# Four changes to the order of work in an attention kernel's first stages: exponentials ahead of a tile's own copy, a product ahead of the projection, reciprocals ahead of the second norm's low half, bias sums on GpSimd

## The chip, the cores and the metric

One core of a Trainium2 chip. The metric is the device time of one execution in microseconds; before the change it is 941.41 us, the median of three runs (941.12 to 943.48).

## The reference, cut to what matters

`x` and `ctx_1024` are (8, 512, 512), float32. Two blocks follow one another, each with a residual:

```python
x = x + xattn(layernorm(x), ctx, ctx, W_proj, b_proj)
x = x + ffn(layernorm(x), wf, uf, bf, wi, ui, bi, wc, uc, bc, wo, uo, bo, in_c)
```

- `xattn`: 16 heads of 32 columns. Scores of queries and keys are scaled by 32 to the power -1/2, masked to a distance of at most 64 positions, put through a softmax and multiplied with the values; `y @ W_proj.T + b_proj` follows.
- `ffn`: a recurrence over the batch axis of 8 steps on a state `c` of (512 rows, 512 columns), starting from `in_c` broadcast to all rows; then the output.

```python
def step(c, xt):
    ft = sigmoid(xt @ wf.T + c @ uf.T + bf)
    it = sigmoid(xt @ wi.T + c @ ui.T + bi)
    gt = tanh(xt @ wc.T + c @ uc.T + bc)
    return ft * c + it * gt, None
h = tanh(x @ wo.T + c_final @ uo.T + bo)
```

## The kernel before, in words

The kernel is one instruction stream for each engine, and all streams walk one list, `steps` (lines 114 to 328). The list is written out by a loop over slots. Each engine takes from it the steps that concern it, in the list's order, and waits on semaphores where it needs another engine's result. So the place of a step in the list is its place in the queue of every engine that does a part of it.

**Tiles and slots.** There are 32 tiles of 128 positions (4 for each of 8 batch elements), and each tile has 4 slots, one for a group of 4 heads: slot n belongs to tile i = n // 4 with s = n % 4. The attention of a slot is made of these steps:

- `score` (PE line 730, 16 small matmuls into the four banks `ps_a`; DVE line 1012 scales, masks and copies to `probs`, and takes the row's minimum, four instructions, one for each head),
- `exp` (ACT line 900, four exponentials, each with its row sum),
- `turn` (PE transposes, lines 742 or 752; ACT line 905 copies the result to `probs_t`; up to slot 19 DVE line 1033 copies a second half),
- `sides` (from slot 20 on: DVE line 1047, 32x32 transposes of what the tile sees of its neighbours),
- `recip` (DVE line 1023, reciprocals of the row sums; POOL line 667 spreads them over the columns of `recip`),
- `value` (PE lines 766, or 773 and 778).

Slots up to 19 are called `early` in the code; from slot 20 on to slot 35 come single slots with products of the recurrence between them; from slot 36 on slots go in pairs.

**Once for each tile.** `ln1`/`ln1b` are the first norm, `bias` (POOL line 647) adds the projection's bias to the row, `query`/`query_out` turn the normed tile. `spread` (s = 3) turns the reciprocals: PE line 796, then ACT line 909 copies them from the bank `ps_m` to `tile_row`. `mult` (DVE line 1054) multiplies the attention's result with them, and `halves` (ACT line 913, POOL line 662) splits the product in a high and a low part. `proj` (s = 0 of the next tile: PE line 805, from tile 5 on lines 683 to 685) is the projection. `resid` and `stat2` (DVE, POOL line 672), then `ln2b` (DVE line 1082) make the second norm. `turn2` (s = 2 of the tile after) turns that normed tile for the recurrence: PE line 820 transposes it into `ps_m`, ACT line 930 copies the high part from there, and DVE line 1098 makes the low part from `ps_m` and the high part, so it waits for ACT's copy.

**The recurrence.** `cell` is one product of three matmuls of 512 columns (lines 683 to 685). 48 of them (12 gates) belong to the first step, from slot 19 on; `gate` (ACT line 947) takes a finished sum, `blend` and `state` follow (DVE, ACT).

**The first step's biases.** The state's share of the first step is the same for all rows. `row` (PE line 788) computes it in slots 5, 13 and 17, `column` (DVE line 1110) turns it to columns in `column_t`, which lies in the tile `gate`, and `column_sum` (DVE lines 1116 and 1119) adds both of its columns to `bias`. The first gate of each kind waits for its own sum (line 942).

**Weights.** `split` (ACT line 936) and `rest` (POOL line 652, two subtractions of 128x512, each) split the gates' weights in the early slots.

The order in a slot, as it matters here (lines 244 to 306):

- early: `turn n`, `exp n+1`, `score n+2`, then for s = 2 `turn2`, `value n`, `column_sum`, `rest`, `recip n+1`.
- slots 20 to 35: `turn n`, two products (a gate behind the first or the second where it ends a sum), then `query`, `turn2` or `spread`, then `score n+2`, `mult`, `exp n+1`, `value n`, `recip n+1`, `sides n+1`; for s = 0 then `ln1b`, `bias`, `proj`, `resid`, `stat2`; and one product at the end.

Two waits tie a slot to the ones around it. A `turn` from slot 20 on writes to the bank `ps_a0`, so PE waits until DVE has taken the first head of the scores of the next slot from it:

```python
pe.wait_ge(masked, HPG * (i + 1) + 1)      # line 749, turn i
```

And `value n` waits for DVE's transposes of `sides n` (line 757), `value` of a tile's first slot also for `mult` of the tile before (line 760).

## Time and profile before

| | |
|---|---|
| median of 3 runs | 941.41 us |
| the profiled execution, its own time | 941.73 us |
| its span, first to last instruction | 939.8 us |
| granted TensorE clock over the span | 1.000, the level of 2.4 GHz |
| PE busy | 919.0 us (98%) |
| DVE busy | 675.9 us (72%) |
| ACT busy | 476.2 us (51%) |
| POOL busy | 204.8 us (22%) |

The profile shows one execution. Busy time of PE counts a matmul from its start to its modelled end, and ends overlap the next start, so gaps between matmuls are seen better in the time from start to start. What ends the time of the kernel is read from waits: the idle time of an engine ahead of an instruction, and the engine that released it.

### The profile page before, as it was taken

To read this page: it belongs to the slowest core of one execution; us is meant where nothing else is said; L and a number is where in the kernel's file an instruction comes from. 1 tells how busy PE (TensorE), PEld (TensorE's weight loads), DVE (VectorE), ACT (ScalarE), POOL (GpSimd) and SP (SyncE) were. 2 spreads that over 40 slices of the span, in tenths; PEclk is the share of its full clock that TensorE was granted. 3 is DMA by queue.
4 is the path that set the end of the run, shared out by engine and by line. 5 is a ranking of instruction groups with operands and counts; after the bars stand their busy time and mean duration, and the time that the engine had idled before them with its cause. 6 is when DMAs were issued, how large, how long until landed. Compare 5 with 4: busy or idle time off the path is not lost.

```text
span 939.8 us, 21981 instructions
## 1 busy us (share of the span) xinstructions
PE 919.0 (98%) x7842; PEld 715.6 (76%) x7842; DVE 675.9 (72%) x2281; ACT 476.2 (51%) x1430; POOL 204.8 (22%) x228
## 2 busy tenths in 40 slices
PE   7999999999999999999999999999999999999998
PEld 5555567677887788887887888788777888888887
DVE  6888898888779977998799878987798531143222
ACT  6888666655565544554465555555555421131222
POOL 5475322211110111111111111111111100003444
PEclk9999999999999999999999999999999999999999
DMA  9564223224443443434543444434333150049862
GB/s 303 163 195 150 85 80 108 74 81 128 133 131 119 129 133 93 140 109 123 133 146 110 119 116 123 108 109 109 98 98 91 50 165 0 1 178 371 324 235 101
DMA packets 139348, 123.58 MB, mean 131 GB/s; under 512 B 46824, under 2 KB 104168, under 8 KB 137704
## 3 DMA queue, kind: packets, MB, share of 16 engines
q1 hardware_dynamic: 138520, 121.91, 42.8%
q8 instruction: 63, 1.03, 0.5%
q10 hardware_dynamic: 720, 0.27, 0.2%
q14 instruction: 45, 0.37, 0.1%
HBM read 87.70 MB, written 34.46 MB: 130 GB/s over the span
## 4 chain that ended last, share of the span: by engine, by line
PE 87%; DVE 6%; issue 3%; ACT 2%; DMA 1%; POOL 1%; SPq 0%; DVEq 0%; POOLq 0%; ACTq 0%
PE ps_g L683 18%; PE ps_g L685 17%; PE ps_g L684 17%; PE ps_a L730 5%; PE ps_a L752 5%; PE ps_m L683 3%; PE ps_v L773 3%; PE ps_m L685 3%; PE ps_m L684 3%; PE ps_m L805 2%; PE ps_a L685 2%; PE ps_a L683 2%; PE ps_a L684 2%; PE ps_v L778 2%; DVE probs L1012 2%
## 5 line engine op out<-in xcount | busy, mean ns | idle before, releaser
L900 ACT ACTIVATE probs<-probs,rowmin 128x192 f32<-128x192 f32 (+1 forms) x512 | 239.4, 470 | 114.4 <-DVE rowmin L1012 114.4
L1012 DVE CUSTOM_DVE_ANT_0 probs<-ps_a,mask 128x192 f32<-128x192 f32 (+1 forms) x512 | 166.0, 386 | 30.0 <-PE ps_a L730 28.8
L683 PE MATMUL ps_g<-state_hi,gate_w 128*128 128x512 f32 x336 | 133.6, 398 | 0.0
L685 PE MATMUL ps_g<-state_hi,gate_w 128*128 128x512 f32 x336 | 131.1, 390 | 0.0
L684 PE MATMUL ps_g<-state_lo,gate_w 128*128 128x512 f32 x336 | 130.8, 389 | 0.0
L1047 DVE STREAM_TRANSPOSE keys<-probs 32x128 f32<-32x128 f32 x420 | 125.6, 299 | 5.2
L947 ACT ACTIVATE gate<-ps_g,bias 128x512 f32<-128x512 f32 x84 | 57.6, 686 | 105.6 <-PE ps_g L685 105.2
L900 ACT ACTIVATION_READ_ACCUMULATOR probs<-probs,rowmin 128x1 f32 x512 | 96.3, 188 | 0.0
L662 POOL TENSOR_TENSOR attn_lo<-recip,attn_hi 128x512 fp32r<-128x512 f32 x23 | 29.8, 1294 | 276.8 <-ACT attn_hi L913 276.8
L905 ACT ACTIVATE probs_t<-ps_a 128x512 f32<-128x512 f32 x108 | 59.3, 595 | 50.9 <-PE ps_a L752 50.9
L683 PE MATMUL ps_g<-x2t_even,gate_w 128*128 128x512 f32 x192 | 80.0, 417 | 0.0
L683 PE MATMUL ps_g<-x2t_odd,gate_w 128*128 128x512 f32 x192 | 76.9, 401 | 0.0
L685 PE MATMUL ps_g<-x2t_even,gate_w 128*128 128x512 f32 x192 | 75.2, 392 | 0.0
L684 PE MATMUL ps_g<-x2t_even,gate_w 128*128 128x512 f32 x192 | 75.0, 391 | 0.0
L685 PE MATMUL ps_g<-x2t_odd,gate_w 128*128 128x512 f32 x192 | 74.9, 390 | 0.0
L684 PE MATMUL ps_g<-x2t_odd,gate_w 128*128 128x512 f32 x192 | 74.8, 390 | 0.0
L685 PEld LDWEIGHTS ps_g<-state_hi,gate_w 128*128 128x128 f32 x336 | 63.1, 188 | 13.4
L683 PEld LDWEIGHTS ps_g<-state_hi,gate_w 128*128 128x128 f32 x336 | 63.1, 188 | 12.6
L684 PEld LDWEIGHTS ps_g<-state_lo,gate_w 128*128 128x128 f32 x336 | 63.2, 188 | 12.3
L730 PE MATMUL ps_a<-keys,queries 32*64 32x192 f32 (+1 forms) x2048 | 62.3, 324 | 2.8 <-DVE rowmin L1012 2.0
L752 PE MATMUL ps_a<-ident,probs 128*128 128x128 f32 x432 | 60.4, 274 | 1.4 <-ACT probs L900 0.7
L752 PEld LDWEIGHTS ps_a<-ident,probs 128*128 128x128 f32 x432 | 51.0, 139 | 13.1 <-ACT probs L900 3.9
(218 smaller groups left out, 1722.6 us busy)
## 6 DMA issues: line engine op xcount, KB each, us to landing
values<-ctx_rows SPq DMA_DIRECT2D x34, 256.0 KB, 4.4
xr<-x SPq DMA_DIRECT2D x32, 256.0 KB, 3.6
keys<-ctx_t SPq DMA_DIRECT2D x16, 512.0 KB, 4.0
x_dram<-xr SPq DMA_DIRECT2D x32, 256.0 KB, 2.6
gate_w<-x2t_dram SPq DMA_DIRECT2D x8, 1024.0 KB, 9.3
keys<-ctx_t SPq DMA_DIRECT2D x16, 384.0 KB, 3.5
x2t_dram<-x2t_even SPq DMA_DIRECT2D x12, 512.0 KB, 4.3
x2t_dram<-x2t_odd SPq DMA_DIRECT2D x12, 512.0 KB, 4.4
```

The source lines that it names most:

```text
L662: pool.tensor_tensor(attn_lo[:, :, :], attn if i < SENT else recip[:, :, :], attn_hi[:, :, :].bitcast(F32), ALU.subtract)\
L683: pe.matmul(ps, lhs[0], rhs[0], start=start, stop=False)
L684: pe.matmul(ps, lhs[0], rhs[1], start=False, stop=False)
L685: return pe.matmul(ps, lhs[1], rhs[0], start=False, stop=stop)
L730: mm = pe.matmul(ps_a[h][q, score_at[i] + k.start:score_at[i] + k.stop], queries[rows, g, q], keys[rows, key_home[tile], g, k], start=True ...
L752: mm = pe.transpose(ps_turn[i][:, h * P:(h + 1) * P], probs[:, i % 2, h, own:own + P], ident[:, :])
L773: pe.matmul(ps_v[HEAD * h:HEAD * (h + 1), g * P:(g + 1) * P], values[:, tile % 2, 0, d], own_home[i][:, h, :], start=True, stop=False)
L900: act.activation(row, row, ACT.Exp, bias=rowmin[:, i % 2, h:h + 1], scale=-1.0, accum_out=rowsum[:, i // G % 2, i % G, h:h + 1]).then_inc( ...
L905: act.activation(own_home[i], ps_turn[i][:, :].rearrange("p (a q) -> p a q", a=HPG), ACT.Copy)\
L947: act.activation(gate[:, min(gt, 1), :], ps_g[i % 2][:, :], ACT.Tanh, bias=(first_bias if b == 0 else bias)[:, gt, m:m + 1], scale=1.0 if ...
L1012: dve.tensor_tensor_reduce(probs[:, i % 2, h, 0:SEEN[t]], ps_a[h][:, score_at[i]:score_at[i] + SEEN[t]], mask[:, MASK0[t]:MASK0[t] + SEEN[ ...
L1047: turn = dve.transpose(side_home[i][BLK * keys_of:BLK * (keys_of + 1), :, q], probs[q, i % 2, :, col:col + BLK])
```

## The change

In the list of steps:

- In the early slots with s = 2, `recip n+1` comes ahead of `turn2` (and so ahead of `column_sum` and `rest` on GpSimd).
- In slots 20 to 35, `exp n+1` comes directly behind the two products, ahead of `query`, `turn2` or `spread`.
- In slots 20 to 35 with s = 0, the product from the slot's end comes ahead of `proj`.

And `column_sum` goes from VectorE (two instructions) to GpSimd (two for the first gate kind, three for the others); every gate of the first step waits for all three sums.

```diff
         elif not early:
             cells(2)
+            if n + 1 < SLOTS:
+                steps.append(("exp", n + 1))
             if s > 0:
                 tile_steps((None, "query", "turn2", "spread")[s], (None, i + 1, i - 1, i)[s])
         if n + 2 < SLOTS:
             steps.append(("score", n + 2))
         if s == 1:
             tile_steps("ln2b", i - 1)
+        recip_first = early and s == 2
+        if recip_first:
+            steps.append(("recip", n + 1))
         if s == 3 and i >= WHOLE:
             tile_steps("mult", i)
         if early:
             tile_steps(("proj", "query", "turn2", "spread")[s], (i - 1, i + 1, i - 1, i)[s])
-        elif n + 1 < SLOTS:
-            steps.append(("exp", n + 1))
...
         if n + 1 < SLOTS:
-            steps.append(("recip", n + 1))
+            if not recip_first:
+                steps.append(("recip", n + 1))
...
             if not early:
+                cells(1)
                 tile_steps("proj", i - 1)
...
         if n >= FIRST_CELL:
-            cells(PER_SLOT[min((n - FIRST_CELL) // (TT * G), B - 1)] - 2)
+            cells(PER_SLOT[min((n - FIRST_CELL) // (TT * G), B - 1)] - (2 if s > 0 else 3))
...
             for kind, i in steps:
+                if kind == "column_sum":
+                    pool.wait_ge(column_turned, i + 1)
+                    pool.wait_ge(bias_half, 1)
+                    row = first_bias[:, i, :]
+                    pool.tensor_tensor(row, column_t[:, :, 0], column_t[:, :, 1], ALU.add).then_inc(column_sum, 1)
+                    pool.wait_ge(column_sum, (1, 2, 4)[i])
+                    if i > 0:
+                        pool.tensor_tensor(row, row, half[:, :].to_broadcast([P, G]), ALU.mult).then_inc(column_sum, 1)
+                        pool.wait_ge(column_sum, (1, 3, 5)[i])
+                        pool.tensor_tensor(row, bias[:, i, :], row, ALU.subtract).then_inc(biased, 1)
+                    else:
+                        pool.tensor_tensor(row, row, bias[:, i, :], ALU.add).then_inc(biased, 1)
...
                     if b == 0:
-                        act.wait_ge(biased, gt + 1)
+                        act.wait_ge(biased, NG)
...
-                if kind == "column_sum":
-                    dve.wait_ge(column_turned, i + 1)
-                    dve.wait_ge(bias_half, 1)
-                    scale = 0.5 if i else 1.0
-                    dve.scalar_tensor_tensor(out=first_bias[:, i, :], in0=column_t[:, :, 0], scalar=scale,
-                                             in1=bias[:, i, :], op0=ALU.mult, op1=ALU.add).then_inc(column_sum, 1)
-                    dve.wait_ge(column_sum, i + 1)
-                    dve.scalar_tensor_tensor(out=first_bias[:, i, :], in0=column_t[:, :, 1], scalar=scale,
-                                             in1=first_bias[:, i, :], op0=ALU.mult, op1=ALU.add).then_inc(biased, 1)
```

## Rows read from the trace of the kernel before

**Rows 1.** Windows by stage; columns: busy us and instructions of each engine, clock, DMA.
```profile
20.00:92.00 72.00, 66.63 (x788) 37.93 (x787) 60.99 (x230) 59.81 (x192) 42.67 (x53) 1.00 0.55 176
92.00:186.00 94.00, 88.28 (x907) 61.75 (x904) 79.92 (x302) 63.08 (x191) 25.20 (x38) 1.00 0.30 86
186.00:700.00 514.00, 512.96 (x4704) 411.31 (x4703) 432.15 (x1477) 274.08 (x861) 81.35 (x83) 1.00 0.43 119
```

**Rows 2.** Waits of PE from 20 to 92 us: us in total, times, longest.
```profile
PE ps_m L796 <- POOL recip L667: 2.3, 4, 1.2
```

**Rows 3.** Waits of PE from 92 to 186 us.
```profile
PE ps_a L752 <- ACT probs L900: 0.7, 4, 0.2
```

**Rows 4.** Waits of DVE from 92 to 186 us.
```profile
DVE probs L1012 <- PE ps_a L730: 5.4, 4, 1.7
DVE x2t_odd L1098 <- ACT x2t_odd L930: 3.7, 4, 1.6
```

**Rows 5.** Timeline, slots 22 and 23: start, us, engine, line, shapes, idle before.
```profile
107.08 0.69 ACT L947 ACTIVATE gate<-ps_g,first_bias 128x512 f32<-128x512 f32 x1
...
108.21 0.60 ACT L930 ACTIVATE x2t_odd<-ps_m 128x512 fp32r<-128x512 f32 x1 [0.44 <-PE ps_m L820]
...
108.71 0.50 ACT L900 ACTIVATE probs<-probs,rowmin 128x256 f32<-128x256 f32 x1
...
108.84 0.69 DVE L1098 TENSOR_TENSOR x2t_odd<-ps_m,x2t_odd 128x512 fp32r<-128x512 f32 x1 [0.17 <-ACT x2t_odd L930]
...
109.20 0.50 ACT L900 ACTIVATE probs<-probs,rowmin 128x256 f32<-128x256 f32 x1
...
109.45 0.41 DVE L1012 CUSTOM_DVE_ANT_0 probs<-ps_a,mask 128x256 f32<-128x256 f32 x1
...
110.21 0.94 PE L752 MATMUL ps_a<-ident,probs 128*128 128x128 f32 x4
```

**Rows 6.** Timeline, slot 24: the sides and the value product behind them.
```profile
117.69 1.85 DVE L1047 STREAM_TRANSPOSE probs_t<-probs 32x128 f32<-32x128 f32 x6
...
119.65 0.42 PE L773 MATMUL ps_v<-probs_t,values 128*32 128x128 f32 x8 [1.20 <-issue]
```

**Rows 7.** Timeline of ACT, slot 30: the first exponential.
```profile
151.81 0.45 ACT L900 ACTIVATE probs<-probs,rowmin 128x192 f32<-128x192 f32 x1
```

**Rows 8.** Timeline, slot 31: gate, spread copy and multiplication.
```profile
155.47 0.69 ACT L947 ACTIVATE gate<-ps_g,first_bias 128x512 f32<-128x512 f32 x1 [0.79 <-PE ps_g L685]
...
156.06 0.59 ACT L909 ACTIVATE tile_row<-ps_m 128x512 f32<-128x512 f32 x1
...
157.56 0.69 DVE L1054 TENSOR_TENSOR tile_row<-ps_v,tile_row 128x512 f32<-128x512 f32 x1
```

**Rows 9.** Timeline of PE, slot 28: start of the projection.
```profile
141.23 0.47 PE L683 MATMUL ps_m<-proj_w,attn_hi 128*128 128x512 f32 x1 [0.29 <-POOL attn_lo L662]
```

**Rows 10.** Timeline of ACT, slot 20: the first gate.
```profile
101.72 0.69 ACT L947 ACTIVATE gate<-ps_g,first_bias 128x512 f32<-128x512 f32 x1 [4.72 <-PE ps_g L685]
```

**Rows 11.** Timeline of DVE, slot 18: the bias sum and the reciprocal behind it.
```profile
89.81 0.15 DVE L1116 SCALAR_TENSOR_TENSOR first_bias<-gate,bias 128x4 f32<-128x4 f32 x1
...
90.07 0.18 DVE L1023 RECIPROCAL invsum<-rowsum 128x4 f32<-128x4 f32 x1
```

**Rows 12.** Timeline, slots 11 and 12.
```profile
56.65 0.66 PE L796 MATMUL ps_m<-ident,recip 128*128 128x128 f32 x4 [1.17 <-POOL recip L667]
...
58.04 0.69 DVE L1054 TENSOR_TENSOR tile_row<-ps_v,tile_row 128x512 f32<-128x512 f32 x1
...
59.31 3.70 PE L805 MATMUL ps_m<-state,tile_row 128*128 128x512 f32 x8
```

**Rows 13.** Lines 667 and 672 on POOL: ns min/median/max, first and last start.
```profile
L667 POOL COPY recip<-invsum x36: 282/292/523, 11.7 to 174.8; 128x128 f32<-128x128 f32 x36
L672 POOL TENSOR_TENSOR moments<-moments,half x32: 549/550/559, 32.8 to 762.1; 128x1 f32<-128x1 f32 x32
```

**Rows 14.** Line 1082 on DVE: ns min/median/max, first and last start.
```profile
L1082 DVE TENSOR_SCALAR tile_row<-xr,moments x32: 543/546/1096, 34.1 to 764.2; 128x512 f32<-128x512 f32 x32
```

## The prediction

> **What bounds the kernel now.** I first cut the span into stages with the windows [rows 1]. From 186 to 700 us PE is busy in 513 of 514 us: there PE alone sets the pace, and whatever an earlier stage gains or loses goes to the end undiminished. The whole change lies ahead of that, in the early slots (20 to 92 us) and the single slots (92 to 186 us). In these two stages PE is idle for 5.4 and 5.7 us, DVE is busy for 85% of both, and ACT for 83 and 67%. So here two or three engines take turns in holding each other up. The views of waits say who. In the early slots PE's largest wait is the transposes of reciprocals, for GpSimd [rows 2]. In the single slots PE waits little for exponentials [rows 3], and DVE waits four times for ACT's copy of the high part, once for each `turn2` (slots 22, 26, 30, 34) [rows 4]. That last row is the one that I look at hardest, because the change puts four exponentials ahead of this copy on ACT.
>
> **Exponentials first, s = 2 (four slots).** Today, in slot 22, ACT does a gate at 107.08, is idle, copies the high part at 108.21 as soon as PE has it, and then does the exponentials at 0.49 us each [rows 5]. DVE takes the low part at 108.84, 0.63 us after the copy began, and the scores of slot 24 behind it, at 109.45. In the list `turn2` stands ahead of `score n+2`, so on DVE nothing passes the low part. With the change ACT starts the exponentials behind the gate (0.60 us from a gate's start to the next one's, [rows 8]): the copy starts 0.60 + 4 x 0.49 = 2.56 us behind the gate's start instead of 1.13. That is 1.43 us later, and so are the low part and all that DVE does after it. (By durations rather than starts it would be 0.69 + 2.0 - 1.13 = 1.56.) In slots 26, 30 and 34 gate and copy start the same 1.13 us apart. In slots 30 and 34 the exponentials have 192 columns and are 0.45 us long [rows 7], by the same overlap 0.44 from start to start: 0.60 + 1.76 - 1.13 = 1.23 us.
>
> Is this on the path? DVE has no gap of 0.1 us between the low part of slot 22 and the end of its transposes in slot 24, at 119.54, and PE stands idle for 1.20 us before the value product at 119.65, which needs them [rows 6]. So the whole 1.43 us reaches PE there. Slot 26 is the same up to slot 28, 1.43 us. There the projection waits 0.29 us for its split operand [rows 9]; the product moved ahead of it covers that, so 1.43 - 0.27 = 1.16 us stay. In slot 30 DVE is 1.23 us late, and a second thing comes on top.
>
> **Exponentials first, s = 3.** In slots 23, 27, 31 and 35 they pass the copy of `spread`, which `mult` needs. In slot 31 the copy starts at 156.06 and `mult` at 157.56 [rows 8]. PE is some 0.8 us late there (below), so the gate starts at 156.27, the exponentials at 156.87, the copy at 158.63, and with its 0.59 us `mult` comes at 159.2, 1.65 us late, more than the 1.23 by which DVE is late anyway. The value product of slot 32 shows no wait for DVE today, so some of that is slack: between 1.23 and 1.65 I take 1.4 us for this tile. In slots 23 and 27 DVE's own delay is the larger, so nothing is added; in slot 35 both give about 1.3 us. What the step wins is that the transposes of a slot wait less for its exponentials: the four of slot 23 are drawn out to 0.94 us [rows 5], of which some 0.3 is waiting. That gain is inside the sum, since PE then waits for DVE instead. Sum of both: 1.43 + 1.16 + 1.4 + 1.3 = 5.3 us lost.
>
> In slots with s = 0 or 1 no ACT work stands between the old place and the new one: zero. The cover is that ACT has only a query copy there, and that stays behind.
>
> **The product ahead of `proj` (s = 0, four slots).** PE does the same work in another order. It fills a wait only in slot 28, counted above. The price is that `resid` gets its sum 0.69 us later (three matmuls of 0.23 us). DVE is idle in these slots before the next scores, four times and 5.4 us together [rows 4], and that hides it; with that gone it would cost up to 0.69 a tile. The first gate comes ahead of `split_proj` on ACT; ACT is idle for 4.72 us before that gate [rows 10]. Zero.
>
> **Bias sums off DVE (slots 6, 14, 18).** Two instructions leave DVE: 89.81 to 90.07 is 0.26 us [rows 11]. In each of these slots DVE works without a gap up to `mult`, on which PE then waits, so 3 x 0.26 = 0.8 us gained. On GpSimd 2, 3 and 3 small additions come in. No row shows one of 128x4; the nearest are the copy of 0.29 us and the power of 0.55 [rows 13]. I take 0.3, so up to 1 us a sum with its waits. Behind them in GpSimd's queue are `rest` and the next `ln1`; the splits that `rest` makes are read by the third row product, three slots later, and SP's loads into the freed buffers are split later still. Zero, and 0.5 us at most. All gates now wait for all three sums, which are made in slot 18, before the first gate at 101.72 [rows 10]. Zero.
>
> DVE instructions can be slowed by GpSimd: the second norm takes 0.55 us as a rule and 1.10 at most [rows 14], the long ones begin while GpSimd subtracts weights. What follows the moved sums on DVE reads PSUM or a single tensor, and such copies and statistics are equally long with and without GpSimd at work beside them, so I add nothing. The Trainium skill, page "SBUF — State Buffer", section "Who interferes with whom", says that GpSimd and a VectorE instruction with two SBUF inputs (or in a two-port mode) exclude one another, the later one blocking fully. By that rule the new additions may hold DVE for their own length, and by it the sums' gain could turn into a loss.
>
> **Reciprocals first (slots 2, 6, 10, 14, 18).** On DVE the reciprocal and the low part change places, which fills 0.1 us in slot 14, where DVE waits for the high part. On GpSimd the spreading no longer stands behind `rest`, and PE's waits for it, 2.3 us in four slots [rows 2], go. Three of them hide behind DVE, which must reach `mult` before the projection can start. In slot 10 it is different: the wait of 1.17 us delays value, transposes and scores one after another, until `proj` at 59.31; `mult` starts at 58.04 and needs 0.62 + 0.05 us, so `proj` could start at 58.7 [rows 12]: 0.6 us gained. Bounds: 0.1 us in all if DVE takes it back, 2.3 if every wait falls out. Sum of the two early parts: 0.8 + 0.1 + 0.6 = 1.5 us gained.
>
> **The sum.** 5.3 - 1.5 = +3.8 us. The profiled execution took 941.73 us (a span of 939.8 and 1.9 around it), 0.3 above the median; 945.5 against it is 945.2 against the median of 941.41. That is 0.4% slower; 0.3%, or 2.8 us, is about what a measurement of this kernel can tell from no change.
>
> **Rivals.**
> - *Turns only* (0.16). DVE catches up in its idle time before the next value product, and PE pays only at the transposes: in slot 23 they need the first masked score, 109.45 + 1.43 + 0.41 = 111.3 instead of 110.21, less the 0.3 us of waits that vanish, 0.8 us. Four times, less 0.3 and 1.5: +1.4, 942.8 us. For it: DVE's longest wait before the low part is 1.6 us [rows 4], so it isn't always full. Against: that idle time lies ahead of the delay, not behind it.
> - *No stall* (0.12). The copy's delay is hidden after all, and the transposes' waits for exponentials, up to 0.3 us in eight slots, are won: -2.4 - 0.3 - 1.5 = -4.2, 937.2 us. This is the side where it is faster. It decides if DVE's low part is not what the next scores wait behind. For it: PE's waits on L900 are real. Against: the order in the list, and rows 4, which show DVE already waiting there.
> - *Nothing moves in the single slots* (0.08): the exponentials, though first in line, find their masked scores late and end as before. Then only the early gain stays, 939.9 us. Against: DVE has those scores done a whole slot earlier.
> - *GpSimd holds DVE* (0.08). At the three sums DVE loses 0.3 us instead of winning 0.26: 945.2 + 3 x 0.56 = 946.9 us. That is the page's rule from above; rows 14 bear out that such blocking occurs here, but for another kind of instruction.
> - The forecast has the rest, 0.56. Its own range is 943.6 (5.3 lost, 0.8 + 2.3 won) to 947.2 (nothing won, and the longer durations).
>
> So slower 0.56 + 0.08, within 0.3% 0.16 + 0.08, faster 0.12. The range of 942.3 to 947.3 us takes in the forecast, the first rival and the last, and leaves out 0.20.
>
> **What the profile after would show.** Right: DVE's wait before L1098 grows from 3.7 to about 9 us; PE gets a wait of about a microsecond at L752 in slots 23, 27, 31 and 35, released by L1012; the wait before the value product of slot 24 grows from 1.2 to some 2 us; the waits of L796 on L667 are gone; L1116 and L1119 run on POOL; from 186 us on all is alike, shifted. Wrong: slot 36 starts earlier than now, the copy L930 starts within 1.2 us of its gate as before, or DVE waits for its high part no longer than now.

## The result, and the profile after

In a comparison of nine executions each, the changed kernel takes 944.61 us in the median (943.93 to 947.66) and the kernel before 941.12 us. The ratio is 1.0041, with a 95% interval from 1.0032 to 1.0051: slower by about 0.4%, more than the 0.3% that can be told from no change. The forecast was 945.2 us, with a range of 942.3 to 947.3.

The profiled execution took 946.33 us (span 944.4 us). It is not the median one, and it began late: its slot 0 already starts 0.88 us behind that of the profile before. Such starts differ from one execution to the next (up to 1.1 us in the profiles below), so all shifts below are counted from slot 0 on. Over the span, PE is busy for 920.0 us, DVE for 674.8, ACT for 476.3 and POOL for 206.1, each within 1.3 us of before. The work is the same; only its order has moved.

The windows by stage, their bounds moved a little with the work (busy us and instructions of PE, PE's weight loads, DVE, ACT and POOL; clock; DMA share and GB/s):

```profile
20.00:91.00 71.00, 67.53 (x804) 38.28 (x796) 60.41 (x227) 59.95 (x194) 44.90 (x61) 1.00 0.55 176
91.00:190.00 99.00, 87.16 (x902) 60.82 (x898) 80.53 (x302) 63.84 (x194) 24.99 (x37) 1.00 0.29 83
190.00:704.00 514.00, 512.84 (x4700) 410.99 (x4696) 431.25 (x1477) 274.14 (x861) 81.53 (x83) 1.00 0.43 118
```

Against [rows 1], PE's idle time fell in the early slots (5.4 us of 72 before, 3.5 of 71 now) and grew in the single slots (5.7 of 94, now 11.8 of 99). From 190 us on there is 1.2 us idle in 514, as before. The waits of DVE and of PE from 90 to 192 us (us in total, times, longest) name the place:

```profile
DVE x2t_odd L1115 <- ACT x2t_odd L947: 8.2, 4, 2.8
DVE probs L1029 <- PE ps_a L747: 2.3, 3, 1.0
DVE tile_row L1013 <- PE ps_m L822: 2.0, 1, 2.0
```

```profile
PE ps_a L769 <- DVE rowmin L1029: 3.5, 4, 1.1
PE ps_a L747 <- ACT probs_t L922: 2.2, 3, 0.8
PE ps_a L769 <- ACT probs L917: 0.5, 3, 0.2
```

Lines of PE, DVE and ACT stand 17 further down than before: L1115 is the low part of `turn2` (L1098 before), L947 ACT's copy of the high part (L930), L769 the transposes (L752), L747 the scores (L730), L1029 DVE's masked scores (L1012). DVE's wait for the copy went from 3.7 us [rows 4] to 8.2, and PE's transposes now wait for DVE, 3.5 us in four slots, where they waited only for exponentials before [rows 3]. DVE's idle time ahead of the masked scores, behind which the working hid several things, shrank from 5.4 us to 2.3. Slot 22 in the timeline (start, us, engine, line, shapes, idle time before and its releaser) is to be read against [rows 5]:

```profile
106.36 0.69 ACT L964 ACTIVATE gate<-ps_g,first_bias 128x512 f32<-128x512 f32 x1
...
106.94 0.50 ACT L917 ACTIVATE probs<-probs,rowmin 128x256 f32<-128x256 f32 x1
...
108.42 0.49 ACT L917 ACTIVATE probs<-probs,rowmin 128x256 f32<-128x256 f32 x1
...
108.91 0.57 ACT L947 ACTIVATE x2t_odd<-ps_m 128x512 fp32r<-128x512 f32 x1
...
109.52 0.69 DVE L1115 TENSOR_TENSOR x2t_odd<-ps_m,x2t_odd 128x512 fp32r<-128x512 f32 x1 [0.86 <-ACT x2t_odd L947]
...
110.13 0.41 DVE L1029 CUSTOM_DVE_ANT_0 probs<-ps_a,mask 128x256 f32<-128x256 f32 x1
...
110.60 0.66 PE L769 MATMUL ps_a<-ident,probs 128*128 128x128 f32 x4 [0.26 <-DVE rowmin L1029]
```

The copy starts 108.91 - 106.36 = 2.55 us behind the gate, where it was 1.13; the working had 2.56. The low part, the masked scores and PE's transposes hang one behind the other as before: the first two steps are 0.6 us apart, and the transposes start 0.5 us behind the first masked score. The transposes have shrunk from 0.94 to 0.66 us: what they waited for exponentials is gone, and in its place they start later. In slot 31 the other half of the move shows, against [rows 8]:

```profile
157.96 0.69 ACT L964 ACTIVATE gate<-ps_g,first_bias 128x512 f32<-128x512 f32 x1 [0.79 <-PE ps_g L702]
...
160.30 0.58 ACT L926 ACTIVATE tile_row<-ps_m 128x512 f32<-128x512 f32 x1
...
160.98 0.69 DVE L1071 TENSOR_TENSOR tile_row<-ps_v,tile_row 128x512 f32<-128x512 f32 x1 [0.49 <-ACT tile_row L926]
```

Gate to copy is 2.34 us instead of 0.59, and `mult` now waits for the copy. In the early slots the wait of [rows 12] is gone, and the sums run on POOL in 0.2 us each (timeline, slots 11 and 18):

```profile
55.90 0.66 PE L813 MATMUL ps_m<-ident,recip 128*128 128x128 f32 x4
...
89.25 0.20 POOL L645 TENSOR_TENSOR first_bias<-gate 128x4 f32<-128x4 f32 x1
```

**Where the time came and went.** The table gives, for each kernel, by how many us ACT's copy behind the transposes of a slot starts later than in the kernel before, less the same number for slot 0. Negative is earlier. The kernels other than "after" are the experiments below; each one's name stands in the heading of its section.

| kernel | slot 14 | 20 | 22 | 24 | 26 | 28 | 30 | 32 | 36 |
|---|---|---|---|---|---|---|---|---|---|
| after | -1.02 | -1.30 | -1.62 | -0.21 | -0.22 | 1.18 | 0.83 | 2.54 | 3.71 |
| no_exp_first | -1.03 | -1.31 | -1.60 | -1.02 | -1.02 | -1.03 | -1.37 | -1.36 | -1.49 |
| exp_first_only | 0.01 | 0.02 | 0.02 | 1.44 | 3.01 | 4.40 | 4.37 | 6.07 | 7.41 |
| exp_first_s2 | -0.99 | -1.27 | -1.56 | -0.15 | 1.32 | 2.71 | 2.38 | 3.50 | 4.50 |
| exp_first_s2_behind | -1.03 | -1.31 | -1.60 | -0.88 | -0.88 | -0.59 | -0.94 | -0.93 | -1.31 |
| exp_first_s3 | -1.01 | -1.29 | -1.58 | -1.01 | 0.59 | 0.85 | 0.53 | 1.46 | 1.82 |
| exp_first_s3_filled | -1.00 | -1.30 | -2.30 | -1.73 | -2.31 | -2.06 | -2.54 | -1.60 | -1.54 |
| turn2_behind_score | -1.02 | -1.31 | -1.61 | -0.89 | 0.58 | 0.86 | 0.52 | 1.16 | 1.20 |
| no_product_ahead | -1.01 | -1.30 | -1.61 | -1.60 | -1.60 | -1.61 | -1.60 | -1.60 | -1.60 |
| product_before_value | -1.03 | -1.31 | -2.31 | -1.73 | -2.33 | -2.33 | -2.81 | -2.81 | -2.72 |
| split_later | -1.00 | -1.30 | -2.30 | -2.29 | -2.88 | -2.88 | -3.36 | -3.36 | -3.25 |
| no_recip_first | -0.36 | -0.56 | -0.87 | -0.29 | -0.29 | -0.30 | -0.64 | -0.63 | -0.75 |
| sums_on_dve | -0.73 | 0.94 | 0.88 | 1.45 | 3.02 | 3.01 | 2.69 | 2.69 | 2.57 |

The changed kernel is 1.3 us ahead at slot 20 and 3.7 us behind at slot 36; from there to slot 80 its shift moves by 0.3 us, and at the end of the span it is 3.7 again. That the later stage passes a shift on unchanged holds here, but not in every kernel: no_exp_first, 1.49 us ahead at slot 36, ends its span 2.7 us ahead. The kernel before has a PE wait of 0.6 us for a second norm at 673 us, which the profiled execution of no_exp_first doesn't have. So a difference between spans of about a microsecond can't be put down to the edited slots alone. A loss comes in each stretch with an s = 2 slot and the slot behind it, and in some stretches PE wins something back (28 to 30: -0.35).

### The profile page after: what moved, and what is told of

The parts are those of the page before. It is cut to its first block, busy times and chain, and to the rows that moved or that the text cites. A ratio compares the mean times of both kernels' runs of the same rounds, so it can differ in the third digit from the quotient of the medians.

```text
span 944.4 us, 21983 instructions
## 1 busy us (share of the span) xinstructions
PE 920.0 (97%) x7842; PEld 716.0 (76%) x7842; DVE 674.8 (71%) x2275; ACT 476.3 (50%) x1430; POOL 206.1 (22%) x236
## 3 DMA queue, kind: packets, MB, share of 16 engines
q8 instruction: 63, 1.03, 0.5%
## 4 chain that ended last, share of the span: by engine, by line
PE 85%; DVE 7%; ACT 3%; issue 3%; DMA 2%; SPq 0%; POOL 0%; DVEq 0%; ACTq 0%
PE ps_g L700 17%; PE ps_g L702 17%; PE ps_g L701 17%; PE ps_a L747 5%; PE ps_a L769 4%; PE ps_m L700 3%; PE ps_v L790 3%; PE ps_m L702 3%; PE ps_m L701 3%; PE ps_m L822 2%; DVE probs L1029 2%; PE ps_a L702 2%; PE ps_a L701 2%; PE ps_a L700 2%; ACT probs L917 2%
## 5 line engine op out<-in xcount | busy, mean ns | idle before, releaser
L1029 DVE CUSTOM_DVE_ANT_0 probs<-ps_a,mask 128x192 f32<-128x192 f32 (+1 forms) x512 | 166.0, 386 | 28.7 <-PE ps_a L747 27.1
L747 PE MATMUL ps_a<-keys,queries 32*64 32x192 f32 (+1 forms) x2048 | 62.7, 325 | 3.9 <-ACT probs_t L922 2.2
L769 PE MATMUL ps_a<-ident,probs 128*128 128x128 f32 x432 | 58.4, 273 | 4.1 <-DVE rowmin L1029 3.5
L769 PEld LDWEIGHTS ps_a<-ident,probs 128*128 128x128 f32 x432 | 50.5, 139 | 15.1 <-DVE rowmin L1029 5.9
```

The lines of the kernel that those rows point to most:

```text
L747: mm = pe.matmul(ps_a[h][q, score_at[i] + k.start:score_at[i] + k.stop], queries[rows, g, q], keys[rows, key_home[tile], g, k], start=True ...
L769: mm = pe.transpose(ps_turn[i][:, h * P:(h + 1) * P], probs[:, i % 2, h, own:own + P], ident[:, :])
L1029: dve.tensor_tensor_reduce(probs[:, i % 2, h, 0:SEEN[t]], ps_a[h][:, score_at[i]:score_at[i] + SEEN[t]], mask[:, MASK0[t]:MASK0[t] + SEEN[ ...
```

## The experiments

The theory was that of the prediction: exponentials passing ACT's copy of the high part hold DVE's low part and the scores queued behind it. The rivals were that the loss comes from the passing of `spread`'s copy, from the product ahead of `proj`, or from GpSimd's new work. Line numbers differ by a few from kernel to kernel; the tiles named in a row tell which step it is. "Before" was measured anew beside each group of kernels: 941.66, 941.58 and 941.86 us.

### All but the exponentials' move (no_exp_first)

```diff
         elif not early:
             cells(2)
-            if n + 1 < SLOTS:
-                steps.append(("exp", n + 1))
...
             tile_steps(("proj", "query", "turn2", "spread")[s], (i - 1, i + 1, i - 1, i)[s])
+        elif n + 1 < SLOTS:
+            steps.append(("exp", n + 1))
```

> The changed kernel with the exponentials of slots 20 to 35 back in their old place; reciprocals first, the sums on GpSimd and the product ahead of the projection stay. Theory (the exponentials delay ACT's copy of the high part, DVE stands still on it, and 5.3 us of the loss is this): only the early gain of 1.5 to 1.6 us and up to 0.3 in slot 28 stay, 939.3 us against 941.1 of before, and DVE waits 3.7 us at the four high parts as before. Rival (the other three parts cost the time, most likely GpSimd's sums holding DVE up): near the changed kernel, 944 us.

Measured: 940.24 us, ratio 0.9986 (0.9977 to 0.9995). The theory had 939.3 us, the rival 944. DVE waits 3.6 us at the high parts, about as before. Slot 36 comes 1.49 us ahead of before instead of 3.71 behind. So the exponentials' move costs 5.2 us of the path, and the other three edits together win 1.5. They don't win it all where the prediction had it: at slot 22 the kernel is 1.60 ahead, at slot 24 only 1.02. The cause is in the timeline of slot 21:

```profile
102.60 0.55 POOL L689 TENSOR_TENSOR moments<-moments,half 128x1 f32<-128x1 f32 x1 [0.44 <-DVE moments L1089]
103.11 2.55 POOL L674 TENSOR_TENSOR proj_w<-state,proj_w 128x512 fp32r<-128x512 f32 x2
...
103.33 0.42 DVE L1029 CUSTOM_DVE_ANT_0 probs<-ps_a,mask 128x256 f32<-128x256 f32 x1
...
104.36 1.58 DVE L1099 TENSOR_SCALAR tile_row<-xr,moments 128x512 f32<-128x512 f32 x1
```

The second norm on DVE takes 1.58 us, three times its usual 0.55 and longer than the 1.10 of [rows 14]. It begins during GpSimd's subtractions of `split_proj` and ends at 105.94, 0.3 us behind their end at 105.66. In the kernel before the two ends stand 0.3 us apart as well (105.95 + 0.86 on DVE, 104.00 + 2.52 on POOL). DVE had its scores done earlier, but the norm could not use that: both times it ends 0.3 us behind GpSimd's second subtraction. The masked scores beside the same subtractions take 0.42 us each, as everywhere else in these slots, so not every DVE instruction is held; split_later below moves the subtractions away and tests the reading.

### Only the exponentials' move (exp_first_only)

```diff
         elif not early:
             cells(2)
+            if n + 1 < SLOTS:
+                steps.append(("exp", n + 1))
...
-        elif n + 1 < SLOTS:
-            steps.append(("exp", n + 1))
```

> The kernel before with the exponentials' move alone. Theory: the whole loss and none of the early gain, +5.3 us or 946.4 us, DVE waits 8 to 9 us at the four high parts. Rival (the other parts cost the time): 941 us, or below it by up to 2.4 us of waits for exponentials.

Measured: 948.44 us, ratio 1.0068 (1.0055 to 1.0082), 7.41 us behind at slot 36; 946.4 us were expected. The first round, slots 22 to 24, costs 1.42 us; the prediction said 1.43. DVE waits 8.9 us for the copy, PE's transposes 4.2 us for DVE. But 1.57 us fall between slots 24 and 26, where no theory had a loss. That is the clock, shown below with exp_first_s3. Without it, 5.8 us: some more than the 5.2 from the other side, since here the norm of slot 21 takes 0.87 us, as in the kernel before, and the first round counts in full: DVE's wait ahead of the low part of slot 22 is 1.58 us, against 0.17 + 1.43 of the prediction.

### Exponentials first, but not in s = 2 (exp_first_s3)

```diff
-            if n + 1 < SLOTS:
+            if s != 2 and n + 1 < SLOTS:
                 steps.append(("exp", n + 1))
             if s > 0:
                 tile_steps((None, "query", "turn2", "spread")[s], (None, i + 1, i - 1, i)[s])
+            if s == 2 and n + 1 < SLOTS:
+                steps.append(("exp", n + 1))
```

> The changed kernel, but in slots with s = 2 the exponentials stand behind turn2 again; in slots with s = 3 they stay ahead of the copy of spread. Theory: DVE's wait at the high part is back to 3.7 us and with it all of the loss goes; ahead of spread the exponentials save up to 0.5 us in each of four tiles: 938 to 939.5 us. Rival (the late copy of spread makes the multiplication late, and that is the loss): 943 to 944 us.

Measured: 943.12 us, ratio 1.0011 (1.0000 to 1.0021). The theory had 938 to 939.5 us, so it missed, and the number is the rival's (943 to 944). DVE's wait for the high part is 3.6 us, as in [rows 4]; so that stall belongs to s = 2 alone. Yet this kernel is 2.9 us slower than no_exp_first. Two waits show why (DVE, then PE, 91 to 190 us; L928 copies the spread reciprocals, L924 the transposed scores):

```profile
DVE tile_row L1073 <- ACT tile_row L928: 1.5, 3, 0.8
```

```profile
PE ps_a L749 <- ACT probs_t L924: 2.4, 3, 0.8
```

Everything that ACT does behind the exponentials is late in the s = 3 slots: the copy for `mult`, the splits, and the next `probs_t`, for which PE's scores wait. Against no_exp_first the stretches 26 to 28, 30 to 32 and 34 to 36 lose 0.27, 0.92 and 0.53 us, 1.7 together. The move was meant to shorten waits here, and in these slots it costs.

The remaining 1.6 us fall between slots 24 and 26 again (-1.01 to 0.59). PE's timeline (some rows left out):

```profile
117.26 0.59 PE L749 MATMUL ps_a<-keys,queries 32*64 32x192 f32 x16 [0.83 <-ACT probs_t L924]
119.05 0.42 PE L792 MATMUL ps_v<-probs_t,values 128*32 128x128 f32 x8 [1.20 <-DVE probs_t L1066]
...
120.99 0.63 PE L702 MATMUL ps_m<-proj_w,attn_hi 128*128 128x512 f32 x1
121.42 0.63 PE L703 MATMUL ps_m<-proj_w,attn_hi 128*128 128x512 f32 x1
...
124.08 0.39 PE L702 MATMUL ps_m<-proj_w,attn_hi 128*128 128x512 f32 x1
124.31 0.39 PE L703 MATMUL ps_m<-proj_w,attn_hi 128*128 128x512 f32 x1
```

And the window from 119 to 124 us (columns as above, the clock behind POOL):

```profile
119.00:124.00 5.00, 4.95 (x28) 3.90 (x29) 4.41 (x17) 1.29 (x3) 0.57 (x2) 0.66 0.00 0
```

Behind two idle stretches of 0.83 and 1.20 us, eight matmuls follow one another at 0.43 us instead of 0.23, and the granted clock of the stretch is 0.66, a mix of 1.2 and 2.4 GHz. 8 x 0.20 = 1.6 us lost. It doesn't happen in each execution. Eight of the eleven have a mean clock of 0.998 and take 942.2 to 944.6 us; the other three (1.000 or 0.999) take 940.7 to 940.9.

### The high part's copy and low part behind the scores (turn2_behind_score)

```diff
-            if s > 0:
+            if s in (1, 3):
                 tile_steps((None, "query", "turn2", "spread")[s], (None, i + 1, i - 1, i)[s])
         if n + 2 < SLOTS:
             steps.append(("score", n + 2))
+        if s == 2 and not early:
+            tile_steps("turn2", i - 1)
```

> The changed kernel, but in slots 22, 26, 30 and 34 turn2 comes behind score n+2 in the list, for PE, ACT and DVE; the exponentials stay ahead of its copy. Theory (what costs is that DVE's scores stand behind the low part's wait, not that the copy is late): DVE does the scores during the exponentials, no stall is left, and the waits for exponentials are won too: 937 to 939.5 us. Rival (the late copy itself costs, since spread must wait for the low part, or ACT is what bounds these slots): 943 to 945 us, with the wait at another instruction.

Measured: 942.05 us, ratio 1.0002 (0.9993 to 1.0011). All exponentials are first here, as in the changed kernel, but on DVE the scores no longer stand behind the low part. The wait shrinks to this:

```profile
DVE x2t_odd L1117 <- ACT x2t_odd L949: 1.2, 3, 0.5
```

Slot 36 is 1.20 us behind before instead of 3.71, and a clock fall of 1.47 us between slots 24 and 26 is in that (the mean clock is 0.997 or 0.998 in seven of eleven executions). Without it slot 36 would be 0.3 us ahead, so the queue behind the low part had cost 4.0 us. That queue was the cause of most of the loss. The median missed the 937 to 939.5 us of the theory: the cost of s = 3 stays, and the clock comes on top.

### Only s = 2 first, in both orders (exp_first_s2, exp_first_s2_behind)

exp_first_s2 is no_exp_first with the exponentials ahead of `turn2`:

```diff
         elif not early:
             cells(2)
+            if s == 2 and n + 1 < SLOTS:
+                steps.append(("exp", n + 1))
...
-        elif n + 1 < SLOTS:
+        elif s != 2 and n + 1 < SLOTS:
             steps.append(("exp", n + 1))
```

> The kernel of no_exp_first with the exponentials ahead of turn2 in slots with s = 2 alone, turn2 ahead of the scores as in the change; it completes the four cases (neither, s = 3, s = 2, both). Theory (DVE's stall at the high part is on the path whole, and behind it the late copy of spread is hidden): 1.43, 1.43, 1.2 and 1.2 us in the four tiles, slot 36 some 5.0 us later than in no_exp_first, or nearly all of what both together lose; 944.3 us. Rival (the two add up, 1.7 us being of spread): 3.5 us later, 942.8 us.

exp_first_s2_behind has the same, and `turn2` behind `score` by the edit of turn2_behind_score:

> The kernel of no_exp_first, and only in slots with s = 2 are the exponentials ahead of turn2, which comes behind score n+2; in slots with s = 3 they stay behind the copy of spread. From turn2_behind_score, which won nothing, and exp_first_s3, which lost 1.5 us beside no_exp_first. Theory (passing the copy of spread makes the multiplication late, in three or four tiles, and passing the high part's copy costs nothing once the scores are ahead of it): at no_exp_first or up to 1 us below it, 938.5 to 939.5 us. Rival (the exponentials ahead of the high part still cost): 941 us.

Measured: 945.11 us, ratio 1.0035 (1.0022 to 1.0049), for the first; 940.55 us, 0.9992 (0.9983 to 1.0000), for the second. The two differ by one place in the list. In the first, the changed kernel's two waits come back to the tenth:

```profile
DVE x2t_odd L1117 <- ACT x2t_odd L949: 8.2, 4, 2.8
```

```profile
PE ps_a L771 <- DVE rowmin L1031: 3.5, 4, 1.1
```

By slot 36 it loses 4.50 + 1.49 = 5.99 us to no_exp_first. 1.47 of it fall between slots 24 and 26, the clock again, so s = 2 costs 4.5 us (0.9 us by slot 24, 1.4 from 26 to 28, 1.1 from 30 to 32 and 1.2 from 34 to 36). The expectation had 5.0 us if the late copy of `spread` hides behind the stall, 3.5 if the two halves add up, so 4.5 lies between the two. The second kernel loses only 0.18 us to no_exp_first by slot 36; its median missed the 938.5 to 939.5 us of the theory, and five of its eleven executions have a mean clock of 0.998. With s = 3 (1.7) the sum of the two halves is 6.2, more than the 5.2 of both together: where DVE is late through s = 2, lateness of `spread` is partly hidden.

### Without the product ahead of the projection (no_product_ahead)

```diff
             if not early:
-                cells(1)
                 tile_steps("proj", i - 1)
...
-            cells(PER_SLOT[min((n - FIRST_CELL) // (TT * G), B - 1)] - (2 if s > 0 else 3))
+            cells(PER_SLOT[min((n - FIRST_CELL) // (TT * G), B - 1)] - 2)
```

> The kernel of no_exp_first (all parts but the exponentials' move) with the product put back behind the projection as well: reciprocals first and the sums on GpSimd alone. In no_exp_first the second norm of slot 21 took 1.58 us beside GpSimd's split of the projection's weights, and 0.7 us of the early gain went there. Theory (the product ahead of the projection delays DVE and GpSimd there, and the norm then waits for GpSimd): the reciprocal of slot 22 comes 1.6 us earlier than before the change instead of 0.9, but slots 28 and 32 win 0.3 and 0.1 us less; time 939.6 us, about that of no_exp_first. Rival (that norm's 1.58 us has nothing to do with the product): slot 22 as in no_exp_first, 0.9 us early, and 0.4 us slower in the end.

Measured, on the basis of no_exp_first: 939.24 us, ratio 0.9979 (0.9970 to 0.9987). The shift stays at -1.60 from slot 22 to 36. So the product ahead costs 0.6 us in slot 20 and wins back 0.35 us in slot 28 and 0.1 in slot 32, where it fills the projection's wait. The way of the loss can be followed: the projection of slot 20 comes 0.7 us later, DVE waits 2.0 us for it (L1013 above; 1.3 in the kernel before), so `stat2` and GpSimd's subtractions behind it come later, and the second norm ends with them. On balance the edit loses 0.1 us of the path. (The medians are 1.0 us apart; four of eleven executions of no_exp_first have a mean clock of 0.998, of this one a single one.)

### Reciprocals back behind; sums back on DVE (no_recip_first, sums_on_dve)

```diff
-        recip_first = early and s == 2
+        recip_first = False
```

> The kernel of no_exp_first with the reciprocals back behind the low half in the early slots. Theory: what they win is in slots 10 to 12 alone, 0.6 us, and a tenth in slot 14, so the lead over the kernel before at the end of slot 12 is 0.3 us instead of 1.0, and the time is 0.7 us above no_exp_first, 940 us. Rival (all of PE's waits of 2.3 us for the reciprocals count): 1.6 us above it, with a loss at each of slots 7, 11, 15 and 19.

Measured: 940.69 us, ratio 0.9993 (0.9983 to 1.0002). From slot 14 on it stands about 0.7 us behind no_exp_first: that is what the reciprocals' place is worth. The sums on GpSimd are left with 0.56 us at slot 20.

The other one puts the two DVE instructions of `column_sum` and the gates' waits back as before the change, and keeps the reciprocals first:

```diff
-                if kind == "column_sum":
-                    pool.wait_ge(column_turned, i + 1)
...
-                        act.wait_ge(biased, NG)
+                        act.wait_ge(biased, gt + 1)
...
+                if kind == "column_sum":
+                    dve.wait_ge(column_turned, i + 1)
```

> The kernel of no_exp_first with the bias sums back on DVE. Theory (0.26 us of DVE's time at each of the three sums is on the path to mult): later by 0.26 us from slot 8 on, 0.5 from slot 16, 0.8 from slot 20, so 0.8 us above no_exp_first, 940.1 us. Rival (GpSimd's two or three additions hold DVE up for as long as the sums took): no difference, or a gain.

Measured: 945.19 us, ratio 1.0037 (1.0023 to 1.0050), where 940.1 was expected: a gain of 0.3 us for each sum can't give the 4.1 us by which slot 36 is later than in no_exp_first. Against no_exp_first, 0.3 us is lost by slot 14 as expected, then 2 us more behind slot 14. Slot 14 in the timeline, POOL and DVE:

```profile
71.49 2.50 POOL L657 TENSOR_TENSOR gate_w<-early_w,gate_w 128x512 fp32r<-128x512 f32 x2
...
71.89 0.90 DVE L1121 SCALAR_TENSOR_TENSOR first_bias<-gate,bias 128x4 f32<-128x4 f32 x1
...
72.82 1.19 DVE L1124 SCALAR_TENSOR_TENSOR first_bias<-gate,first_bias 128x4 f32<-128x4 f32 x1
...
73.94 0.67 DVE L1038 COPY probs_t<-ps_g 64x512 f32<-64x512 f32 x1
```

Two additions on four columns take 0.90 and 1.19 us. In the kernel before they took 0.15 and 0.16 in all three slots, and here they do so in the other two. In the kernel before, the pair of subtractions of this slot ended at 72.47, just ahead of the first sum at 72.55. With the reciprocals first, GpSimd starts its pair of subtractions (71.49 to 73.99) just ahead of them; the first sum ends at 72.79, where the first subtraction should end (71.49 + 1.25 = 72.74), and the second at 74.01, with the second subtraction. Then DVE's `probs_t` is late, and the value product waits 1.7 us for it. So the reciprocals' move needs the sums' move. At slot 20 the sums' move alone gives -0.56 us, the reciprocals' move alone +0.94, and both -1.31. (The further 1.6 us between slots 24 and 26 is the clock again; its mean is 0.996 to 0.998 in all five executions.)

The Trainium skill, page "SBUF — State Buffer", section "Who interferes with whom", says that a VectorE instruction with two SBUF inputs and a GpSimd one that reads SBUF exclude each other, and that the one that starts later is fully blocked. These rows agree with it, in duration and in where the blocking ends.

### Another place for the product (product_before_value, exp_first_s3_filled)

```diff
             steps.append(("exp", n + 1))
+        if s == 0 and not early:
+            cells(1)
         if n < SLOTS:
             steps.append(("value", n))
...
             if not early:
-                cells(1)
                 tile_steps("proj", i - 1)
```

> The kernel of no_exp_first, but the product that was moved ahead of the projection goes one step further, ahead of value n in slots 20, 24, 28 and 32. PE stands idle there for 1.5, 1.2, 0.3 and 0 us. Theory: its 0.69 us fill that idle time in slots 20 and 24 and 0.3 in slot 28, the projection of slot 20 isn't delayed any more, and TensorE's clock falls less often behind the shorter idle time: about 1.5 us below no_exp_first, 938 us. Rival (DVE's transposes bound these slots, and the projection behind has to wait for its split operand instead): as no_exp_first, 939.3 us.

Measured, on the basis of no_exp_first: 938.36 us, ratio 0.9968 (0.9956 to 0.9981), slot 36 at -2.72; 938 was expected. PE used to be idle ahead of the value products of the s = 0 slots (slot 24 in [rows 6]); the same three matmuls fill that time there, and the wait of 1.20 us in slot 24 is down to 0.31.

The same edit on exp_first_s3 tests the reading of the clock, since it fills the idle 1.20 us ahead of the fall:

> The kernel of exp_first_s3 with the product that stood ahead of the projection moved on ahead of value n, into PE's idle time. In exp_first_s3 PE stood idle for 0.8 and 1.2 us in slot 24, and in 8 of 11 runs the clock was granted at 0.998 of full speed; in the profiled one it was at 1.2 GHz for 3.4 us just behind that idle time, and 1.6 us were lost. Theory (the idle time brings the clock down): granted clock 1.000 or 0.999 in nearly all runs, and 2.5 to 3 us below exp_first_s3, 940 to 940.6 us. Rival (the clock falls whatever PE does there): 0.998 as often as before, and only the 1.3 us of the filled wait won, 941.8 us.

Measured: 939.82 us, ratio 0.9978 (0.9969 to 0.9987), 3.3 us below exp_first_s3. All eleven executions have a mean clock of 1.000 or 0.999. The same window as above, and PE's wait ahead of the value product of slot 24:

```profile
119.00:124.00 5.00, 5.00 (x34) 3.84 (x39) 4.83 (x16) 2.04 (x9) 1.59 (x2) 1.00 0.00 0
```

```profile
117.89 0.43 PE L793 MATMUL ps_v<-probs_t,values 128*32 128x128 f32 x8 [0.30 <-issue]
```

The wait of 0.83 us ahead of the scores is still there; that of 1.20 us is down to 0.30, and the clock stays at 2.4 GHz. Of the 3.36 us between the two profiled executions at slot 36, 1.6 are the clock's, and the rest came with the work that was moved into the gap. By whole executions the rest is smaller: the three of exp_first_s3 at a mean clock of 0.999 or 1.000 are about 1 us above the median here.

The other runs bear the reading out. With the second wait filled (exp_first_s3_filled, product_before_value, split_later) none of 21 executions has a mean clock below 0.999. In every kernel whose profile shows that wait at its 1.20 us, some have. How many goes only roughly with the wait ahead of the scores: 9 of the 70 executions of the kernel before that were measured beside the experiments (0.37 us), 4 of 11 of no_exp_first (0.60), 8 of 11 of exp_first_s3 (0.83), but also all five of sums_on_dve (0.59) and only two of nine of the changed kernel (0.83). So the first wait doesn't decide alone, and why one execution falls and the next doesn't stays open.

### GpSimd's subtractions a slot later (split_later)

On top of product_before_value, the second pair of `split_proj` moves on GpSimd (not on ACT) to the slot behind:

```diff
         if FIRST_CELL <= n < FIRST_CELL + 2:
-            steps.append(("split_proj", PAIR * (n - FIRST_CELL)))
+            steps.append(("round_proj", PAIR * (n - FIRST_CELL)))
+        if n in (FIRST_CELL, FIRST_CELL + 2):
+            steps.append(("split_proj", n - FIRST_CELL))
...
-                if kind == "split_proj":
+                if kind == "round_proj":
                     if i == 0:
                         act.wait_ge(wp_in, DMA)
```

> The kernel of product_before_value, and GpSimd's second pair of subtractions for the projection's weights comes a slot later (ACT's half of it stays). In every kernel so far the second norm of slot 21 on DVE ran into them: 0.86 us in the kernel before, 1.58 in no_exp_first, 0.55 elsewhere. Theory (GpSimd's reads hold that norm up): it takes 0.55 us, and slot 24 comes 0.3 us earlier than in product_before_value: 938.0 us. Rival (it is something else, or the subtractions then hold up the next instruction with two SBUF inputs): the norm as long as before, or the same time at another instruction, 938.4 us or more.

Measured: 937.97 us (937.77 to 938.27), ratio 0.9961 (0.9949 to 0.9974), the lowest median of all. In slot 21:

```profile
103.67 0.54 DVE L1102 TENSOR_SCALAR tile_row<-xr,moments 128x512 f32<-128x512 f32 x1
...
104.62 2.53 POOL L677 TENSOR_TENSOR proj_w<-state,proj_w 128x512 fp32r<-128x512 f32 x2
```

The norm takes 0.54 us instead of 1.58, and slot 24 comes 0.56 us earlier than in product_before_value. So it was GpSimd's subtractions that held the norm. (The expectation's "0.55 elsewhere" is not right: in each kernel four norms of the early slots, beside subtractions too, take 0.6 to 1.1 us, as [rows 14] has for the longest.) It beats both the kernel before and the changed one: slot 36 is 3.25 us earlier than before, the profiled span 3.4 us shorter (936.4 against 939.8), and by the two ratios, 0.9961 and 1.0041, it takes 0.8% less than the changed kernel. Against product_before_value it is not shown to be faster as a whole. The medians differ by 0.4 us, less than the intervals can tell. In the profiled executions it leads by 0.53 us at slot 36, but its span is 0.5 us longer (936.4 against 935.9): from 600 to 700 us PE has the wait of the kernel before again, which product_before_value hasn't:

```profile
PE ps_m L840 <- DVE tile_row L1102: 0.6, 1, 0.6
```

## Why the prediction was right

**Exponentials first, s = 2: right, in mechanism and size.** The copy came 1.42 us later (1.43 predicted), and taken alone (exp_first_only) the first round cost 1.42 us. Behind that the changed kernel lost 1.4 us between slots 26 and 28 and 1.35 between 34 and 36, where the working had 1.43 and 1.3. With the other edits the first round's price was only 0.8 us (-0.21 against -1.02 at slot 24), for a reason that the prediction lacked: DVE's wait ahead of the low part was 0.86 us and not 0.17 + 1.43, because GpSimd had held DVE in slot 21 and a part of the copy's lateness was hidden by that. So "the whole 1.43 us reaches PE there" held for the move alone, not for the whole change. *Turns only* (0.8 us a round) fell with the 1.42 us of exp_first_only, *no stall* with DVE's wait of 8.2 us; turn2_behind_score shows that it is the scores queued behind the low part that cost.

**Exponentials first, s = 3: the direction right, the size a little low.** In slot 31 the copy stands 2.34 us behind the gate, 2.36 predicted. Slots 30 to 32 lost 1.71 us; of the bounds 1.23 and 1.65 I took 1.4, and the upper one held. The gain that was put into the sum for the transposes (0.3 us each) is real and pays nothing: PE waits for DVE and ACT in its place. Total of the move: 5.2 us. The prediction's 5.3 has the product's 0.27 us already taken off, so in like terms it is 5.2 against 5.6 us.

**The product ahead: the "zero" for its price was wrong.** It cost 0.6 us behind slot 20, by way of `stat2`, GpSimd and the second norm. The working called `resid`'s delay of 0.69 us hidden by DVE's idle time, and did not follow the result on to GpSimd, which starts its subtractions behind it. The gain for the projection's wait was 0.35 + 0.1 us instead of 0.27. In all the edit lost 0.1 us where the prediction had a gain of 0.27.

**Sums and reciprocals: the total right.** 1.5 us were predicted by slot 20, and there the reciprocals come 1.6 us earlier, PE's work 1.3. Its split was close as well, as long as the sums go first: 0.8 for the sums (measured in no_recip_first: 0.56 in PE's work at slot 20, 0.85 at its reciprocals), 0.7 for the reciprocals on top (0.75). What it missed is that the parts don't add: reciprocals first, with the sums left on DVE, cost 0.9 us instead of winning 0.7, by a blocking that the working had looked for only in the other direction. The rival *GpSimd holds DVE* looked at GpSimd's new additions, which are 0.2 us long and held nothing: the low parts and copies of `probs_t` beside them take 0.65 to 0.69 us, as before. (None of these has two SBUF inputs, so whether one that has would have been held stays open.) Blocking mattered in the other direction, for the old sums behind subtractions that had moved, and for the second norm.

**What the profile was to show.** DVE's wait before the low part: "about 9 us", 8.2. The waits on the spreading are gone. PE's wait at the transposes, "about a microsecond" in each of four slots: 3.5 us in four. Only the value product of slot 24 did not go from 1.2 to 2 us. It stayed at 1.20; PE was already late by then, having waited 0.26 us at slot 23's transposes, 0.33 ahead of its value product, and 0.83 ahead of the scores, for ACT's copy, where it had waited 0.37 before. That last wait was not foreseen.

**The sum.** -1.3 at slot 20, +5.0 from there to 36: 3.7 us, against 3.8 predicted; the ratio gives 0.0041 x 941.1 = 3.9 us, with an interval from 3.0 to 4.8. In the prediction's terms: early parts -1.6 (by slot 22; -1.5 predicted), the product +0.1 (-0.27), the exponentials +5.2 (+5.6). The mechanism is the predicted one, but that the sum came out within 0.1 us is in part luck: the norm held in slot 21 cost 0.6 us and made the first round 0.6 cheaper, and the dearer s = 3 of slot 31 (0.3 more) stands against a larger gain of the product (0.2 more). The clock took no part in the profiled execution, where the granted clock of the single slots is 1.00; in two of the nine it was 0.998, and these took 946.5 and 947.7 us.

## What to carry to other kernels

When a step is moved ahead on one engine, look for the one instruction that a second engine has queued behind what was passed: here a copy that came 1.4 us later held not only its own reader but the scores behind that reader, and one exchange of two list entries took away some 4 us of the loss. Fill idle time of the bounding engine where it stands (ahead of the value product), rather than at the next place where order allows. And check what GpSimd does during a small VectorE instruction before moving either: a sum of 0.15 us can cost over a microsecond.

## What was not expected of the hardware

- **The clock can fall behind two short waits.** Behind idle stretches of 0.83 and 1.20 us of PE the granted clock went to 1.2 GHz for eight matmuls, 1.6 us lost, in some executions and not in others; in sums_on_dve, behind 0.59 and 1.20. Filling the second took it away in all 21 executions of three kernels. Whether filling the first would do as well was not tried. The changed kernel has the same two waits, and its profiled execution no fall.
- **Some VectorE instructions begun during a GpSimd subtraction end with it**, or 0.3 us behind it, whatever their own size: the two bias sums (0.15 to 0.90 us, 0.16 to 1.19) and the second norm (0.55 to 1.58). Masked scores (0.42 us), low parts (0.69) and copies out of PSUM (0.68) that begin during such subtractions keep their time. The norm has a single tensor as its input, and its scalars come from SBUF; why it is held was not tested.
- **Small GpSimd instructions are cheap.** 128x4 additions and products take 0.20 us, where the copy of [rows 13] takes 0.29 and the power 0.55.
- **The start of an execution** (to slot 0) differed by up to 1.1 us between profiled executions with the same early work.
